# A fused two-level graph network: products with the activation's high part first in three places, and a new order of the first steps

## The reference

```python
xn = _layernorm(x, axis=-1)
x = x + _L0_gnn_ref(xn, ...) + _L0_mix_ref(xn[None], ...)[0]
x = x + _L0_ffn_ref(_layernorm(x, axis=-1)[None], ...)[0]
xn = _layernorm(x, axis=-1)
x = x + _L1_gnn_ref(xn, ...) + _L1_mix_ref(xn[None], ...)[0]
x = x + _L1_ffn_ref(_layernorm(x, axis=-1)[None], ...)[0]
```

## Time and profile before

| | |
|---|---|
| runs | 808.17, 806.64, 808.11 us; median 808.11 |
| span of the profiled execution | 807.4 us (its own run time is not listed; the median of the runs is 0.7 us above the span) |
| TensorE busy | 776.9 us, 96% of the span |
| weight loads busy | 687.6 us, 85% |
| VectorE busy | 587.1 us, 73% |
| ScalarE busy | 387.0 us, 48% |
| mean granted clock | 0.995 |

### The profile page before, as it was taken

The page is one execution under the profiler, slowest core; times in us unless marked ns, Lnnn a source line. Parts: engine busy times, 40 slices in busy tenths (PEclk is TensorE's granted clock), DMA queues, the critical chain, the costliest instruction groups (busy, mean ns, idle before and its releaser), DMA issues. The chain is left out here.

```text
span 807.4 us, 11521 instructions
## 1 busy us (share of the span) xinstructions
PE 776.9 (96%) x4268; PEld 687.6 (85%) x4270; DVE 587.1 (73%) x1240; ACT 387.0 (48%) x800; POOL 48.7 (6%) x88
## 2 busy tenths in 40 slices
PE   5999999999999899999997699999999999999998
PEld 4888878889999899998875388888888879999886
DVE  8988888645554788997699959789896677675331
ACT  5222123454443676775767546575674333464220
POOL 3000000000000000001102211000002020000000
PEclk9999999999999999999999999999999999999999
DMA  5522123332434322329965439334135136334341
GB/s 187 184 79 79 53 70 140 130 124 85 130 106 150 98 73 92 99 59 318 271 245 113 129 85 265 102 110 157 53 105 133 64 117 151 130 131 147 127 131 39
DMA packets 28775, 102.17 MB, mean 127 GB/s; under 512 B 3736, under 2 KB 3864, under 8 KB 28464
## 3 DMA queue, kind: packets, MB, share of 16 engines
q1 hardware_dynamic: 24784, 86.76, 31.9%
q0 software_dynamic: 3936, 14.68, 8.4%
HBM read 91.99 MB, written 1.57 MB: 116 GB/s over the span
## 5 line engine op out<-in xcount | busy, mean ns | idle before, releaser
L1191 DVE TENSOR_TENSOR w_lo<-raw,w_hi 128x1024 fp32r<-128x1024 f32 x140 | 169.8, 1221 | 65.0 <-ACT w_hi L901 64.3
L901 ACT ACTIVATE w_hi<-raw 128x1024 fp32r<-128x1024 f32 x140 | 147.3, 1058 | 104.8 <-PE bank L1950 82.4
L1898 PE MATMUL bank<-xn1T,w_hi 128*128 128x384 f32 x448 | 115.2, 338 | 0.0
L1950 PE MATMUL bank<-w_hi,xn3T 128*128 128x512 f32 x288 | 92.0, 393 | 0.0
L1898 PEld LDWEIGHTS bank<-xn1T,w_hi 128*128 128x128 f32 x448 | 79.9, 188 | 1.0 <-DVE w_lo L1191 0.2
L1898 PE MATMUL bank<-xn1T,w_lo 128*128 128x384 f32 x224 | 75.0, 335 | 0.0
L1898 PE MATMUL bank<-xn4T,w_hi 128*128 128x384 f32 x256 | 65.2, 335 | 0.3 <-DVE xn4T L1182 0.3
L1950 PEld LDWEIGHTS bank<-w_hi,xn3T 128*128 128x128 f32 x288 | 54.1, 188 | 11.0
L1950 PE MATMUL bank<-w_lo,xn3T 128*128 128x512 f32 x144 | 56.0, 389 | 0.0
L1898 PEld LDWEIGHTS bank<-xn4T,w_hi 128*128 128x128 f32 x256 | 46.1, 188 | 0.6 <-issue 0.6
L1898 PE MATMUL bank<-xn4T,w_lo 128*128 128x384 f32 x128 | 42.8, 335 | 0.0
(11 more groups left out here) (353 smaller groups left out, 1688.3 us busy)
## 6 DMA issues: line engine op xcount, KB each, us to landing
raw<-weights SPq DMA_DIRECT2D x140, 512.0 KB, 3.3
row_sb<-rows SPq DMA_DIRECT2D x6, 512.0 KB, 5.7
kcat<-kcat POOLq DMA_DIRECT2D x16, 192.0 KB, 2.8
base<-rows POOLq DMA_DIRECT2D x6, 512.0 KB, 13.1
w2r<-w_in SPq DMA_DIRECT2D x1, 2048.0 KB, 10.3
w1r<-w_in POOLq DMA_DIRECT2D x1, 2048.0 KB, 9.8
x_sb<-x_in SPq DMA_DIRECT2D x3, 512.0 KB, 5.1
row_sb<-rows SPq DMA_DIRECT2D x6, 256.0 KB, 4.8
```

The lines of the kernel that those rows point to most:

```text
L901: act.activation(w_hi[:, u % RING], raw[:, u % RAW], ACT.Copy).then_inc(hi_split, 1)
L1191: dve.tensor_tensor(w_lo[:, u % RING], raw[:, u % RAW], f(w_hi[:, u % RING]), ALU.subtract).then_inc(unit_split, 1)
L1898: last = pe.matmul(out_of(pr)[:, 0:N], w[pa][:, slot, k * P:(k + 1) * P], TT[src][:, pb, k], start=(k == 0 and m == 0), stop=(k == KD - 1 ...
L1950: last = pe.matmul(out_of(pr)[:], tile[:, pa, k, ts], w[pb][:, at_, j * HALF:(j + 1) * HALF], start=(kk == 0 and j == 0 and m == 0 and nam ...
```

## The change

The number and size of the operations stay as they are. v1.0, v1.1 and e1.0 get an order of passes of their own, in which the passes with the activation's high part need only the ScalarE copy (`act_hi`) of a chunk, and those with low weights only then wait for the low half of the weight. The tiles of g1 do all products with the high part of two units first, then those with the low part, and the transposes of tile 2 come one step later. On VectorE one of four dead-edge steps stays ahead of the third tile's normalisation and three go behind it, and the split of unit 0 goes behind the first low chunk. On SP, bias and tiny go behind the first three weight loads.

```diff
-    ... tiled("g1", 0, 0, 2, 4), ("x_norm", 2), ("xn3_T", 2),
-                  tiled("g1", 0, 1, 0, 2), ("xn3_hi", 2), ("xn3_lo", 2), tiled("g1", 0, 1, 2, 4), ("g1_out", 0),
+    ... tiled("g1", 0, 0, 2, 4), ("x_norm", 2),
+                  tiled("g1", 0, 1, 0, 2), ("xn3_T", 2), ("xn3_hi", 2), ("xn3_lo", 2), tiled("g1", 0, 1, 2, 4), ("g1_out", 0),
...
-            sp.dma_start(bias[:], cols).then_inc(small_landed, 16)
-            sp.dma_start(tiny_sb[:], tiny.partition_broadcast(P)).then_inc(small_landed, 16)
...
+                    if u == RAW - 1:
+                        sp.dma_start(bias[:], cols).then_inc(small_landed, 16)
+                        sp.dma_start(tiny_sb[:], tiny.partition_broadcast(P)).then_inc(small_landed, 16)
...
-            dead_edges(0)
+            dead_edges(0, 0, 1)
             link(dve.tensor_tensor(cls[:], cls[:], chunk_no[:], ALU.add))
-
+            layer_norm(x_sb, xn1, NT - 1)
             note(dve.tensor_scalar(power[:], cls[:], 8388608.0, None, ALU.mult))
-            layer_norm(x_sb, xn1, NT - 1)
-            split_up_to(0)
+            dead_edges(0, 1, 4)
...
                         chunk_lo(s[1], k, f"{s[1]}.{k}")
+                        if s[1] == "xn1" and k == 0:
+                            split_up_to(0)
...
+            HIGH_FIRST = {("v1", 0): (((HI, HI),), ((LO, HI),), ((HI, LO),)), ("v1", 1): (((HI, HI),), ((HI, LO),), ((LO, HI),)),
+                          ("e1", 0): (((HI, HI), (LO, HI)), ((HI, LO),))}
...
+                        wait_bank(pe, pr)
+                        pe.wait_ge(hi_split, u + 1)
+                        if name == "e1":
+                            wait_split(pe, u)
+                        for ps in HIGH_FIRST[(name, i)]:
+                            if (LO, HI) in ps:
+                                wait_split(pe, u)
+                            for k in range(KD):
+                                if i == 0:
+                                    if (HI, LO) in ps:
+                                        wait_emptied(pe, f"{FEATURE_MAJOR[name]}.{k}")
+                                    else:
+                                        pe.wait_ge(act_hi, hi_at[f"{FEATURE_MAJOR[name]}.{k}"])
+                                for pa, pb in ps:
+                                    last = pe.matmul(out_of(pr)[:, 0:N], w[pa][:, slot, k * P:(k + 1) * P], tile[:, pb, k], ...)
+                        last.then_inc(unit_done, 1)
+                        continue
...
-                        if name == "g1" and n == 0:
-                            wait_bank(pe, pr)
-                            wait_emptied(pe, f"xn3.{t}.0")
-                            wait_emptied(pe, f"xn3.{t}.1")
+                        if name == "g1":
+                            if n == 0:
+                                wait_bank(pe, pr)
+                            pe.wait_ge(act_hi, hi_at[f"xn3.{t}.{2 * n // KH}"])
+                            for k in (2 * n, 2 * n + 1):
+                                for part in (HI, LO):
+                                    pe.matmul(out_of(pr)[:], TT[src][:, HI, k, ts],
+                                              w[part][:, u % RING, (k % 2) * HALF:(k % 2 + 1) * HALF], ...)
+                            continue
...
+                    for n in range(first, end) if name == "g1" else ():
+                        wait_emptied(pe, f"xn3.{t}.{2 * n // KH}")
+                        for k in (2 * n, 2 * n + 1):
+                            last = pe.matmul(out_of(pr)[:], TT[src][:, LO, k, ts], w_hi[...], start=False, stop=(k == KD - 1))
+                        if t == NT - 1:
+                            last.then_inc(unit_done, 1)
```

More of the change, by code:

```diff
@@ L186, in schedule @@
     run("g1", 0, 4)
-    steps.extend([tiled("g1", 0, 0, 0, 2), ("xn3_T", 1), ("xn3_hi", 1), ("xn3_lo", 1), tiled("g1", 0, 0, 2, 4), ("x_norm", 2), ("xn3_T", 2),
-                  tiled("g1", 0, 1, 0, 2), ("xn3_hi", 2), ("xn3_lo", 2), tiled("g1", 0, 1, 2, 4), ("g1_out", 0),
+    steps.extend([tiled("g1", 0, 0, 0, 2), ("xn3_T", 1), ("xn3_hi", 1), ("xn3_lo", 1), tiled("g1", 0, 0, 2, 4), ("x_norm", 2),
+                  tiled("g1", 0, 1, 0, 2), ("xn3_T", 2), ("xn3_hi", 2), ("xn3_lo", 2), tiled("g1", 0, 1, 2, 4), ("g1_out", 0),
                   tiled("g1", 0, 2, 0, 2), tiled("g1", 0, 2, 2, 4), ("g1_out", 1), ("ahead",), ("ahead",), ("g1_out", 2)])
@@ L627, in gps_kernel @@
         block = ctx.enter_context(nc.Block())
+        hi_at = {}
         def f(ap):
@@ L895, in hi_part @@
                 hi[0] += 1
+                if name:
+                    hi_at[name] = hi[0]
             def split_unit(u):
@@ L1296, in expert_split, with dead_edges @@
                 dve.tensor_tensor(tile[:, 1, i % KD], hf[:, i % 2], f(tile[:, 0, i % KD]), ALU.subtract).then_inc(h_scaled, 1)
-            def dead_edges(q):
+            def dead_edges(q, first=0, end=4):
                 pr = f"keys.{q}"
                 wait_full(dve, pr)
-                for j in range(4):
+                for j in range(first, end):
                     c = 4 * q + j
@@ L1885, in _ @@
                         continue
-                    wait_split(pe, u)
                     w = (w_hi, w_lo)
                     slot = u % RING
+                    if (name, i) in HIGH_FIRST:
+                        tile, pr = TT[FEATURE_MAJOR[name]], f"{name}.{i}"
+                        wait_bank(pe, pr)
[12 more added lines that the diff above has]
+                                for pa, pb in ps:
+                                    last = pe.matmul(out_of(pr)[:, 0:N], w[pa][:, slot, k * P:(k + 1) * P], tile[:, pb, k],
+                                                     start=(k == 0 and (pa, pb) == (HI, HI)),
+                                                     stop=(k == KD - 1 and (pa, pb) == HIGH_FIRST[(name, i)][-1][-1]))
+                        last.then_inc(unit_done, 1)
+                        continue
+                    wait_split(pe, u)
                     if name in FEATURE_MAJOR:
@@ L2028, in _ @@
                             wait_split(pe, u)
-                        if name == "g1" and n == 0:
-                            wait_bank(pe, pr)
-                            wait_emptied(pe, f"xn3.{t}.0")
-                            wait_emptied(pe, f"xn3.{t}.1")
+                        if name == "g1":
[5 more added lines that the diff above has]
+                                    pe.matmul(out_of(pr)[:], TT[src][:, HI, k, ts],
+                                              w[part][:, u % RING, (k % 2) * HALF:(k % 2 + 1) * HALF],
+                                              start=(k == 0 and part == HI), stop=False)
+                            continue
                         for j in range(2):
@@ L2041, in _ @@
                         elif kk == per - 1:
+                            full(last, pr)
+                    for n in range(first, end) if name == "g1" else ():
+                        wait_emptied(pe, f"xn3.{t}.{2 * n // KH}")
+                        for k in (2 * n, 2 * n + 1):
+                            last = pe.matmul(out_of(pr)[:], TT[src][:, LO, k, ts],
+                                             w_hi[:, UNIT_OF[(name, n)] % RING, (k % 2) * HALF:(k % 2 + 1) * HALF],
+                                             start=False, stop=(k == KD - 1))
+                        if t == NT - 1:
+                            last.then_inc(unit_done, 1)
+                        elif n == TILED - 1:
                             full(last, pr)
```

## The result

Before: median 808.14 us (806.63 to 809.01, 10 runs). After: median 805.25 us (803.07 to 805.51, 10 runs). The ratio is 0.9966 with an interval of 0.9958 to 0.9975: faster by 2.0 to 3.4 us, 2.9 in the medians, about a third of a per cent. The runs of both kernels fall into two groups. After: eight runs between 805.09 and 805.51, the other two at 803.07 and 803.55. Before: six between 808.11 and 809.01, four between 806.63 and 806.77. Upper group against upper and lower against lower, the middle values differ by 3.3 and 3.4; the median of before lies at the low edge of its upper group, and so the medians show less.

The account below looks back on a forecast made before the run. TensorE was taken to set the pace nearly everywhere, but not at three edited places. Gains of 2.0 + 1.55 - 0.05 (g1), 0.4 (e1) and 0.1 (front) sum to 4.0: 808.1 to 804.1 us, range 802.4 to 805.8.

Parts of the forecast that it names:

- The offset: Whole kernel: the runs' median, 808.11, lies 0.7 above the profiled span, 807.4, and this carries over unchanged.
- g1: 2.0 + 1.55 - 0.05: g1: first product 2.0 earlier, half-clock stretch gone for 1.55, 0.05 lost waiting for tile 1's normalised rows.
- rival (d): g1: TensorE starts early but stands at tile 1's transposes or a low part; 807.1 if it took 3; chance 0.06.
- The rule on transposes: Ahead of g1: if transposes do not count as busy, the low clock could stay, 805.6; given a small chance only.
- rival (a): g1: the clock falls all the same, so 1.55 is missing: 805.6; chance 0.14.
- e1.0: 0.4: e1.0: high-part passes need only ScalarE's copies, whose last one sets the bound; 0.4 earlier.
- The front: 0.1: Front: third tile's transposes 0.7 earlier, mostly eaten by the pace of ScalarE's copies; 0.1 at most won.
- SP's order: SP's queue at the front: weight 0 is asked for sooner; worth nothing by itself.
- (e): q units: q.0's split comes 0.9 later, against 1.6 of cover; with two whole loads lost, 810.9; chance 0.05.
- (c): Outside g1, such as at 274: one half-clock stretch less, 802.5; chance 0.08.

Follow-up runs that it names:

- before_warm: Kernel before plus matmuls with unread results filling TensorE's idle gaps ahead of attend 0, in the FFN and ahead of g1; 805.46 us, ratio 0.9968.
- high_warm: g1_warm with the old step list: high-part-first g1 tiles, but tile 2's transposes stay ahead of tile 1's first half; 807.26 us, ratio 0.9994.
- g1_only: Kernel before with only the g1 part of the change (moved transposes and high-first tiles); 803.75 us, ratio 0.9954.
- after_again: Kernel after, unchanged, timed again on another chip; 803.91 us, ratio 0.9955.
- g1_again: g1_only, unchanged, timed again on the chip of after_again; 805.27 us, ratio 0.9964.
- g1_warm: g1_only plus the filling matmuls of after_warm, so without the front and e1.0 parts; 803.53 us, ratio 0.9950.
- after_warm: Kernel after plus matmuls with unread results in TensorE's gaps ahead of attend 0 and in the FFN, none ahead of g1's first product; 803.18 us, ratio 0.9938.
- e1_banks_warm: after_warm with e1.0 and e1.1 exchanged between their PSUM banks, so e1.0 writes the bank holding xn4's chunk 1; 804.09 us, ratio 0.9954.
- sp_only: Kernel before with only bias and tiny moved behind the first three weight loads on SP's queue; 808.0 us, ratio 1.0006.
- front_only: Kernel before with only the front part: v1.0 and v1.1 high part first, VectorE's new order, SP's new order; 807.45 us, ratio 0.9996.
- step_warm: before_warm with only the transposes of xn3 tile 2 moved behind the first half of g1's tile 1; 805.89 us, ratio 0.9978.

## Why the prediction was right or wrong, point by point

**Forecast.** Faster, 804.1, in a range of 802.4 to 805.8: the sign, the place and the range were right, the time was 1.15 low, and the gain, 4.0, was 2.9 in the medians. In spans I said 803.4 and the profiled execution has 803.7. That this is so near is partly luck: the 0.5 that I counted for e1.0 and the front was not there, the FFN took 0.66, and what made up for them were 0.49 by an earlier first transpose, which follows no edit, and 0.28 in B.

**The offset.** I carried over 0.7 between the median of the runs and the span. All runs of the experiments, which are listed with their span, have 1.7 to 1.8. The profiled execution of before was thus one of about 809.1, above all ten of its runs and 1.0 above their median, and the sum made on it was 1.0 too low as a run's time; this is most of the 1.15. Counted as gains, the same miss reads: 0.5 for two terms that were not there, and 0.6 more, most of which the two groups of runs make (like group with like, the gain is 3.3 to 3.4 and not 2.9).

**g1: 2.0 + 1.55 - 0.05.** Right: D gave 2.03 (start 458.46, forecast 458.55) and E 1.57, tile 1's transposes came at 461.30 (461.3), and the low part was never waited for. I put all of the 1.55 down to the clock. With the clock alone mended (before_warm) E gives 1.39, and the other 0.2 comes only with the moved transposes. The predicted place of tile 2's rows held too (transposes at 467.67, forecast 467.7), but I named the moved transposes as one condition among several ("wanted at 467.7, because the tile-1 products now stand ahead of that transpose"). high_warm shows what hung on it: all of the 2.0 and 1.8 more. That is my rival (d), TensorE early and then standing at a transpose because the norm chain is no faster; I gave it 0.05 of wait in this change, which was right, and did not say what keeps it away.

**The rule on transposes.** From 457.08 to 458.46 TensorE did nothing but eight transposes and then waited 0.34, and g1 ran at a clock of 1.00. So it did behind the same start in the profiled executions of g1_only, after_again, g1_again, g1_warm, after_warm and e1_banks_warm. So rival (a) did not come, though its 805.6 is nearer to the measured 805.25 than the forecast: the profiled execution has its lower clock at 274 and in the FFN, not in g1. The Trainium skill (TensorE: Matmul & The Clock Gate, Part 4: PE-mode transpose) says that transposes do not count as busy for the clock in the same way. The traces do not bear it out. That a high clock stays high shows, besides in g1, in the stage of xn4's transposes in before,

```profile
660.03 0.39 PE L1861 MATMUL bank<-ident,xn_nat 128*128 128x128 f32 x2
661.04 1.69 PE L1861 MATMUL bank<-ident,xn_nat 128*128 128x128 f32 x12 [0.63 <-DVE x_sb L1491]
...
663.74 1.31 PE L1861 MATMUL bank<-ident,xn_nat 128*128 128x128 f32 x10 [1.01 <-DVE xn_nat L1221]
```

where TensorE runs nothing else from 660.2 to 665.4 and the granted clock is 1.00, as at this place in all fourteen profiled executions. That a low clock rises behind transposes alone shows at the front, which I overlooked. TensorE's first rows in g1_only are

```profile
4.69 1.01 PE L1823 MATMUL bank<-ident_h,key_part 128*128 128x128 f16 x8 [4.69 <-DVE key_part L1341]
9.18 3.37 PE L1866 MATMUL bank<-ident,xn_nat 128*128 128x128 f32 x14 [3.47 <-ACT xn_nat L942]
12.87 1.31 PE L1866 MATMUL bank<-ident,xn_nat 128*128 128x128 f32 x10 [0.32 <-DVE xn_nat L1226]
```

and the same last ten transposes in high_warm

```profile
13.06 2.18 PE L1870 MATMUL bank<-ident,xn_nat 128*128 128x128 f32 x10 [0.33 <-DVE xn_nat L1226]
```

In g1_only the first fourteen start 0.21 apart and the last ten 0.11, as fast as the ten at 663.74 above (1.31 too), with nothing but transposes on TensorE since 9.18; in high_warm the last ten are still 0.21 apart. The clock row says 1.00 for all of this, but the trace has no clock record ahead of its first one, a rise to 1.00, at 12.78 in g1_only and at 14.89 in high_warm; the pace shows the lower level before it.

**e1.0: 0.4.** Wrong. I freed the start from VectorE because the pass reads only the activation's high part, and took ScalarE's last copy as the bound. e1.0 writes bank 0, which holds xn4's chunk 0 until VectorE's first subtraction has read it, and all eight banks hold chunks of xn4, so none is free. The start moved by 0.09 at most (F 184.93 against 185.02), and the 24 products then take what they took (G 4.30 against 4.24). e1_banks_warm shows that the bank holds the start. (For e1.0 the new code also waits for the weight's low half ahead of all passes, not only ahead of those that read it; this was not what it stood on.)

**The front: 0.1.** Nothing measurable, for the reason given: the third tile's transposes did come sooner and without a wait, at 12.30 (forecast 12.6), which is 3.16 behind the first transpose where it was 3.69, v1.0 began 5.15 behind the first transpose instead of 5.43, and its first eight products took 1.98 instead of 1.39, the pace of ScalarE's copies that I had counted on. But v1.1 began 9.90 behind the first transpose, where it began 9.72 behind it before. A is 14.07 against 14.02. One execution cannot tell 0.1 there: when TensorE's pace doubles at the front differs from one to the next, at 14.44 in before, behind the last transpose in after, and at 12.46 in e1_banks_warm, whose A of 13.79 is the lowest.

**SP's order and (e).** sp_only takes what before takes, within its interval, and q.0 began without a wait: the 0.9 was inside its cover.

**(c), and what I did not have.** I gave one half-clock stretch less elsewhere a chance of 0.08 and did not see that the stretches are a property of the execution: after loses 1.1 or more at 274 and 0.7 in the FFN in its profiled execution and neither in that of after_again, the same kernel: about half of the change's effect.

**A version that beats both.** after_warm: 803.18, 5.2 under before on its chip and 0.7 under after_again, with nothing but surplus matmuls added to the kernel after; its five runs no longer fall into two groups.

## What to carry to other kernels

When one product is let start earlier, follow the engine's queue to the next instruction that needs something from another chain, and ask whether that has become earlier too; if not, put ready work ahead of it, or the gain turns into a wait there. A pass that reads only what one engine writes is freed from another engine only if its output bank is free as well. Where the clock falls behind TensorE's idle gaps, as it did here in some executions behind gaps of some 2 us, compare two kernels with the gaps filled, stage by stage; their medians alone mix the edit with the stretches.

## What the hardware showed that I had not expected

- A half-clock stretch is not fixed by the program. Ahead of 274 TensorE was busy 0.89, 0.81 and 0.94 of 3 us in before, after and front_only, idle for 2.19 in one piece each time, and the clock behind it was 0.50, 0.54 and 1.00. In g1, behind a gap of 2.3, it came in all four profiled executions that had the gap.
- Cost of one stretch: 1.39 in g1 (E, 19.82 to 18.43), 1.1 to 2.2 at 274 (B, 410.55 to 410.83 against 408.64 to 409.48), 0.4 to 0.7 in the FFN (C, 23.11 and 23.32 against 22.67 to 22.69), where TensorE waits for other engines in between.
- Filling TensorE's gaps made no stage longer (C 22.69, D 3.40 in before_warm) and narrowed the times: spreads of 0.6 (before_warm, six runs) and 0.7 us (after_warm, five), against 2.3 for ten runs of before on the same chip. It does not do so always: step_warm, filled like before_warm, spread over 1.9.
- xn1's first transpose comes at 9.09 to 9.63 in these executions, in no order with the edits.
- TensorE begins at its lower pace, and transposes alone bring it up: 0.21 apart at first, 0.11 from 12.87 on in g1_only. When it rises differs between executions (the first clock record stands at 12.46 to 15.42).
